# Who begins the base layer's loads: from SyncE's queue to ScalarE's, at the head of its program

## The chip, the cores and the metric

One core of a Trainium2 chip runs the kernel. The metric is the device time in microseconds (us) of one execution; it is given as the median of several runs. The engines are TensorE (PE; its weight loads are PEld), VectorE (DVE), ScalarE (ACT), GpSimd (POOL) and SyncE (SP). "SPq" and "ACTq" are the places where SyncE and ScalarE issue DMAs. The core has 16 DMA engines.

## What is computed

Two layers over x (8 sequences of 512 tokens, 512 wide), each added to its input. The first, cut to what matters:

```python
ae = layernorm(cond, ln_g, ln_b)                 # cond is 8 x 512
h  = gelu(ae @ w1 + b1)
xw = h @ w2 + b2                                 # two factors of rank 8 for each sequence
layer = base_layer[None] + einsum('bdr,bkr->bdk', x_a, x_b)
x = x + (x + einsum('btc,bco->bto', x, layer))
```

The second takes the result: a shared gated network (silu(x w1) * (x w3)) w2, and a router that picks 2 of 8 experts for each token; each expert is gelu(x W1e) W2e. Their weighted sum, divided by 3, is added to x.

`base_layer` is a 512 x 512 matrix in float32 (1 MB). The kernel adds 2 to its diagonal, which takes the two additions of x into the same product.

## The kernel before, in words

Each engine has a program written out by hand, and semaphores tie them together. Every float32 operand of a large product is cut into a high part (a cast to fp32r on ScalarE) and a low part (a subtraction on VectorE); a product is then three matmuls: high by high, low by high, high by low.

Batch b of x is loaded in four tiles of 128 tokens, `xtok[:, t]`, 256 KB each. For each tile TensorE turns it with four transposes (`xtr`, L1478) into a PSUM bank; ScalarE casts that to `xTh` (`xt_hi_`, L799) and VectorE makes `xTl` (`xt_lo_`, L1106). Batch b of the first layer is `base_half(b, o, half)` (L1493 to L1495): for each of four output chunks o, two halves of six matmuls with `bh`, `bl` and the turned x.

The base layer comes in four loads of 256 KB, `basep[:, k]`. VectorE waits for all four (`base_in`), adds 2 to the four diagonal blocks (L1136), ScalarE casts each to `bh` (L838), and VectorE subtracts to get `bl` (L1140). The first half of `base_half(0, 0)` needs all four `xTl` of batch 0 and two `bl`; the second half needs four. Later `turn_base` (L1564) reads `basep` again.

What sets the order around the change:

- SyncE's program begins with three small loads (`craw`, `lng`, `lnb`; L507), then x's four loads of batch 0 (L509), then the four of the base layer (L511), then `w1c` (1 MB), the router weights `rwr`, `rbias`, `b2v` and `cb1T` (L517, L519), the first two 2 MB pieces of `w2c` (L524), the next batch of x (L528), and so on.
- ScalarE's program begins with a square root for the layer norm (L833), before which it loads its function table, and which waits for `stats` from VectorE (`D_VAR`). Then come the four `xt_hi_` of batch 0 and the four casts of `bh`.
- VectorE's program begins with the statistics of `craw` (L1121 to L1123), the reciprocal and two operations on `ae` (L1128 to L1130), the four `xt_lo_` of batch 0, and only then the wait for `base_in`, the four diagonal adds and the four `bl`.
- TensorE's program begins with transposes of `craw` (L1469), the sixteen transposes of batch 0, and `base_half(0, 0)`. The small net on `ae` (L1586) and the conditioning network (`cond_net`, L1555, eight pieces of `w2c`) are put between the following `base_half` calls.
- GpSimd makes constants from `upper` (L702) on once `bl` is there.

Much later, SyncE loads the shared network's weights in pieces of 512 KB into one buffer, `wraw` (L488); ScalarE and VectorE cut each into its parts (L792, L1100) before the next is begun.

Of the kernel before, what the change touches and what calls it, by code (L numbers as in the profile page):

```python
# [14 lines left out]
P = 128  # L15
# [10 lines left out]
def build(nc, x, cond, base, cw1, cb1, cw2, cb2, ln_g, ln_b, rw, rb, w1, w3, w2, w1e, w2e, out):  # L26
    NB, T, D = x.shape
    KC = D // P
    TT = T // P
    HS = w1.shape[1]  # L30
    HC = HS // P
    E, _, HE = w1e.shape
    RK = cw2.shape[1] // (2 * D)
    N = NB * T
# [50 lines left out]
    with ExitStack() as ctx:  # L85
        def sb(name, shape, dt=F32, where=ctx):
            return where.enter_context(nc.sbuf_tensor(name, shape, dt))

        def sem(name):
            return ctx.enter_context(nc.semaphore(name))  # L90
# [113 lines left out]
        with ExitStack() as st:  # L204
# [16 lines left out]
            with ExitStack() as z:  # L221
                basep = sb("basep", [P, KC, D], F32, z)
# [25 lines left out]
        base_in = sem("base_in")  # L248
# [255 lines left out]
        def _(sp):  # L504
# [2 lines left out]
                sp.dma_start(dst, src).then_inc(small_in, 16)  # L507
            for t in range(TT):
                sp.dma_start(xtok[:, t], x_view[:, t, :]).then_inc(x_in[t], 16)  # L509
            for k in range(KC):  # L510
                sp.dma_start(basep[:, k], base[k * P:(k + 1) * P, :]).then_inc(base_in, 16)  # L511
            for dst, src in ((w1c[:], cw1.rearrange("(k p) n -> p k n", p=P)),
                             (rwr[:], rw.rearrange("(k p) e -> p k e", p=P)),
                             (rbias[:], row_bc(rb, P)),
# [273 lines left out]
        def _(act):  # L788
# [39 lines left out]
            def exp_scores(g):  # L828
                act.wait_ge(z_sb, g + 1)
                nc.scalar.activation(ex[:], zx[:], ACT.Exp, scale=-1.0).then_inc(ez, 1)  # L830

            act.wait_ge(d0, D_VAR)
            nc.scalar.activation(stats[:, 9:10], stats[:, 8:9], ACT.Sqrt).then_inc(a0, 1)  # L833
            for t in range(TT):
# [987 lines left out]
```

## Time and profile before

| | us |
|---|---|
| three runs: lowest, median, highest | 1112.78, 1113.86, 1113.91 |
| the profiled execution: span from first to last instruction | 1114.8 |
| TensorE busy in it | 1075.8 (97%) |
| VectorE, ScalarE, GpSimd busy | 483.5, 398.6, 154.2 |
| first base matmul starts | 13.01 |

The profiled execution is one execution; of its own time only the span is shown. It lies 0.9 us above the median of the three runs. Times in the profile count from the span's start. "Busy" of an engine is the time in which it ran instructions other than waits and DMA issues. A row of the timeline gives start, duration, engine, line and operation, and in brackets the idle time before it with what ended it; a row "x4" merges four in a row.

### The profile page before, as it was taken

To read this page: it belongs to the slowest core of one execution; us is meant where nothing else is said; L and a number is where in the kernel's file an instruction comes from. 1 tells how busy PE (TensorE), PEld (TensorE's weight loads), DVE (VectorE), ACT (ScalarE), POOL (GpSimd) and SP (SyncE) were. 2 spreads that over 40 slices of the span, in tenths; PEclk is the share of its full clock that TensorE was granted. 3 is DMA by queue.
4 is the path that set the end of the run, shared out by engine and by line. 5 is a ranking of instruction groups with operands and counts; after the bars stand their busy time and mean duration, and the time that the engine had idled before them with its cause. 6 is when DMAs were issued, how large, how long until landed. Compare 5 with 4: busy or idle time off the path is not lost.

```text
span 1114.8 us, 15416 instructions
## 1 busy us (share of the span) xinstructions
PE 1075.8 (97%) x5226; PEld 878.4 (79%) x5226; DVE 483.5 (43%) x1014; ACT 398.6 (36%) x687; POOL 154.2 (14%) x193
## 2 busy tenths in 40 slices
PE   7999899899699999999999999999999999999998
PEld 5666678688488888888888888888888888888886
DVE  3103654463356646655664533331424333142434
ACT  3212344351366566656656631211212121121211
POOL 2002267370000000000000022011020201102020
PEclk9999899999899999999999999999999999999999
DMA  8662589789768688767657445023050501305041
GB/s 308 263 255 72 187 296 395 277 295 306 204 191 263 210 246 267 223 191 218 203 152 201 174 135 205 1 60 129 0 188 0 188 0 59 130 0 188 0 151 38
DMA packets 131702, 191.42 MB, mean 172 GB/s; under 512 B 9534, under 2 KB 73022, under 8 KB 129878
## 3 DMA queue, kind: packets, MB, share of 16 engines
q1 hardware_dynamic: 120118, 156.38, 43.8%
q0 software_dynamic: 11552, 34.61, 8.3%
q8 instruction: 20, 0.33, 0.1%
q14 instruction: 12, 0.10, 0.0%
HBM read 117.04 MB, written 73.92 MB: 171 GB/s over the span
## 4 chain that ended last, share of the span: by engine, by line
PE 86%; DVE 5%; DMA 4%; SPq 3%; ACT 1%; issue 1%; DVEq 0%; ACTq 0%
PE K L1464 10%; PE K L1465 10%; PE K L1466 10%; PE L L1466 5%; PE L L1464 5%; PE L L1465 5%; PE Rb L1466 5%; PE Rb L1464 5%; PE Rb L1465 5%; PE M L1464 4%; PE M L1466 4%; PE M L1465 4%; PE Rb L1555 3%; PE M L1493 2%; PE M L1495 2%; PE M L1494 2%
## 5 line engine op out<-in xcount | busy, mean ns | idle before, releaser
L462 ACT ACTIVATE slf<-K 128x512 f32<-128x512 f32 x64 | 38.3, 598 | 219.7 <-PE K L1466 219.0
L775 POOL DMA_INDIRECT yb<-ys_d,pos_fix x64 | 61.3, 958 | 321.4 <-DVE total L1395 253.3
L465 ACT CAST gTh<-slf 128x512 fp32r<-128x512 f32 x64 | 39.8, 621 | 183.0 <-DVE slf L475 183.0
L1464 PE MATMUL M<-w2h,gTh 128*128 128x512 f32 x256 | 99.7, 389 | 0.5 <-DVE gTl L477 0.5
L1464 PE MATMUL K<-x1h,w13h 128*128 128x512 f32 x256 | 99.7, 389 | 0.0
L1466 PE MATMUL K<-x1h,w13l 128*128 128x512 f32 x256 | 99.6, 389 | 0.0
L1465 PE MATMUL M<-w2l,gTh 128*128 128x512 f32 x256 | 99.6, 389 | 0.0
L1466 PE MATMUL M<-w2h,gTl 128*128 128x512 f32 x256 | 99.6, 389 | 0.0
L1465 PE MATMUL K<-x1l,w13h 128*128 128x512 f32 x256 | 99.6, 389 | 0.0
L475 DVE TENSOR_TENSOR slf<-L,slf 128x512 f32<-128x512 f32 x32 | 22.1, 691 | 155.9 <-PE L L1466 150.8
L1332 DVE TENSOR_TENSOR e2l<-e2raw,e2h 128x512 fp32r<-128x512 f32 x64 | 41.3, 687 | 79.3 <-ACT e2h L929 79.3
L475 DVE TENSOR_TENSOR slf<-Rb,slf 128x512 f32<-128x512 f32 x32 | 22.1, 691 | 117.8 <-PE Rb L1466 117.8
L754 POOL DMA_INDIRECT xs_d<-x1tok,pos_int x64 | 65.5, 1023 | 35.4 <-issue 18.8
L1336 DVE TENSOR_TENSOR hTl<-hg,hTh 128x512 fp32r<-128x512 f32 x64 | 44.1, 689 | 59.0 <-ACT hTh L945 59.0
L477 DVE TENSOR_TENSOR gTl<-slf,gTh 128x512 fp32r<-128x512 f32 x64 | 44.3, 692 | 47.5 <-ACT gTh L465 47.5
L1493 PE MATMUL M<-xTh,bh 128*128 128x512 f32 x128 | 56.8, 444 | 6.8 <-DVE bl L1140 4.0
L769 POOL COPY pos_fix<-ypos 128x8 int32 (+1 forms) x8 | 1.5, 190 | 446.5 <-DMA ys_d<-yo 405.9
L1464 PE MATMUL K<-x1h,e1h 128*128 128x512 f32 x128 | 50.6, 396 | 11.1 <-DVE x1l L1322 11.1
L1464 PEld LDWEIGHTS M<-w2h,gTh 128*128 128x128 f32 x256 | 48.1, 188 | 10.9 <-DVE gTl L477 1.0
L1466 PEld LDWEIGHTS K<-x1h,w13l 128*128 128x128 f32 x256 | 48.1, 188 | 10.0
L1466 PEld LDWEIGHTS M<-w2h,gTl 128*128 128x128 f32 x256 | 48.0, 188 | 10.0
L1465 PEld LDWEIGHTS K<-x1l,w13h 128*128 128x128 f32 x256 | 48.1, 188 | 9.9
(248 smaller groups left out, 2469.4 us busy)
## 6 DMA issues: line engine op xcount, KB each, us to landing
w2c<-in_L_cond_w_dram SPq DMA_DIRECT2D x8, 2048.0 KB, 8.4
e1raw<-in_L_cond_W1e_dram SPq DMA_DIRECT2D x16, 1024.0 KB, 7.2
e2raw<-in_L_cond_W2e_dram SPq DMA_DIRECT2D x16, 1024.0 KB, 5.6
xr<-xs_d SPq DMA_DIRECT2D x64, 256.0 KB, 4.6
ys_d<-yo SPq DMA_DIRECT2D x32, 512.0 KB, 7.3
xtok<-in_x_dram SPq DMA_DIRECT2D x32, 256.0 KB, 7.4
x_d<-x1tok SPq DMA_DIRECT2D x8, 1024.0 KB, 8.1
xs_d<-zeros SPq DMA_DIRECT2D x8, 1024.0 KB, 8.4
```

The costliest lines, as they stand in the source:

```text
L462: nc.scalar.activation(slf[:, h % 2], U[h % 2][:], ACT.Silu).then_inc(ffn.silu, 1)
L465: nc.scalar.copy(gTh[:, h % 2], slf[:, h % 2]).then_inc(ffn.g_hi, 1)
L475: nc.vector.tensor_tensor(slf[:, h % 2], V[h % 2][:], slf[:, h % 2], ALU.mult).then_inc(ffn.g_f, 1)
L477: nc.vector.tensor_tensor(gTl[:, h % 2], slf[:, h % 2], gTh[:, h % 2].bitcast(F32), ALU.subtract).then_inc(ffn.g_lo, 1)
L754: pool.indirect_dma_start(out=xs_d, out_offset=bass.IndirectOffsetOnAxis(ap=pos_int[:, c:c + 1].bitcast(U32), axis=0), in_=x1tok[i][:, t, ...
L775: pool.indirect_dma_start(out=yb[:, c, :], out_offset=None, in_=ys_d, in_offset=bass.IndirectOffsetOnAxis(ap=pos_fix[:, c:c + 1].bitcast(U ...
L1332: tt(e2l[:, m], e2raw[:, m], e2h[:, m].bitcast(F32), ALU.subtract).then_inc(e2_lo, 1)
L1336: tt(hTl[:, m], hg[:, m % 2], hTh[:, m].bitcast(F32), ALU.subtract).then_inc(ht_lo, 1)
L1464: mm(o, ah, bh_, start=start, stop=False)
L1465: mm(o, ah, bl_, start=False, stop=False)
L1466: return mm(o, al, bh_, start=False, stop=stop)
L1493: mm(bank[:], bh[:, c, cols], xh[:, c], start=(c == 0), stop=False)
```

## The change

The loop of four `dma_start` for `basep` is taken out of SyncE's program, where it stood between x's loads and `w1c`, and put at the head of ScalarE's program, ahead of the wait for `stats` and the square root. Sources, destinations and the semaphore are the same.

```diff
@@ block.sync
             for t in range(TT):
                 sp.dma_start(xtok[:, t], x_view[:, t, :]).then_inc(x_in[t], 16)
-            for k in range(KC):
-                sp.dma_start(basep[:, k], base[k * P:(k + 1) * P, :]).then_inc(base_in, 16)
             for dst, src in ((w1c[:], cw1.rearrange("(k p) n -> p k n", p=P)),
@@ block.scalar
+            for k in range(KC):
+                act.dma_start(basep[:, k], base[k * P:(k + 1) * P, :]).then_inc(base_in, 16)
             act.wait_ge(d0, D_VAR)
             nc.scalar.activation(stats[:, 9:10], stats[:, 8:9], ACT.Sqrt).then_inc(a0, 1)
```

The head of ScalarE's program in the changed kernel (the first row is the jump into the program):

```order
L785 UNCONDITIONAL_BRANCH
L831 DMA basep<-in_L_cond_base_layer_dram 128x512 x4
L833 ACT_TABLE_LOAD
L833 ACTIVATE stats<-stats 8x1
L797 CAST xTh<-K 128x4x128 x2
L797 CAST xTh<-M 128x4x128 x2
```

The four issues stand ahead of the table load, and the rest of ScalarE's rows follow in their old order; the line numbers between the two places of the edit are lower by two.

The head of SyncE's program as a difference:

```order
 L507 DMA lnb<-in_L_cond_ln_b_dram 8x512
 L509 DMA xtok<-in_x_dram 128x512 x4
-L511 DMA basep<-in_L_cond_base_layer_dram 128x512 x4
-L517 DMA w1c<-in_L_cond_w_dram 128x4x512
-L517 DMA rwr<-in_L_cond_router_W_dram 128x8x8
+L515 DMA w1c<-in_L_cond_w_dram 128x4x512
+L515 DMA rwr<-in_L_cond_router_W_dram 128x8x8
```

On SyncE `w1c` now follows x's four loads directly, and all that stands behind it moves up by the four issues. The rows of TensorE and VectorE are the same in both kernels.

## Rows read from the trace of the kernel before

**Rows 1.** The page: span, busy time of each engine, and the chain's shares.
```profile
span 1114.8 us, 15416 instructions
...
PE 1075.8 (97%) x5226; PEld 878.4 (79%) x5226; DVE 483.5 (43%) x1014; ACT 398.6 (36%) x687; POOL 154.2 (14%) x193
...
PE 86%; DVE 5%; DMA 4%; SPq 3%; ACT 1%; issue 1%; DVEq 0%; ACTq 0%
```

**Rows 2.** The chain in order of time, 0 to 60 us: start, duration, what.
```profile
1.93 0.36 SPq L509
...
3.75 0.43 SPq L511
...
5.18 5.39 DMA basep<-n_L_cond_base_layer_dram
10.59 0.30 DVE basep L1136
10.92 0.63 ACT bh L838
11.57 1.30 DVE bl L1140 x2
13.01 0.76 PE M L1493
13.77 0.43 PE M L1494
...
17.18 0.24 PE M L1493
17.42 0.23 PE M L1494
...
21.17 4.04 PE L L1586 x32
```

**Rows 3.** The timeline of ScalarE and VectorE from 0 to 14 us.
```profile
0.80 1.28 ACT L833 ACT_TABLE_LOAD   x1 [0.80 <-PEq L1809]
...
3.19 0.68 DVE L1121 BATCH_NORM_STATS2 stats<-craw 8x6 f32<-8x512 f32 x1 [3.19 <-DMA lnb<-in_L_cond_ln_b_dram]
...
4.28 0.20 ACT L833 ACTIVATE stats<-stats 8x1 f32<-8x1 f32 x1 [2.20 <-DVE stats L1123]
...
9.65 0.69 DVE L1106 TENSOR_TENSOR xTl<-M,xTh 128x512 fp32r<-128x512 f32 x1 [0.44 <-ACT xTh L799]
10.59 0.90 DVE L1136 SCALAR_TENSOR_TENSOR basep<-ident,basep 128x128 f32<-128x128 f32 x4 [0.25 <-DMA basep<-n_L_cond_base_layer_dram]
```

**Rows 4.** The line L509, x's first four loads: durations and landing times of the issues.
```profile
L509 SPq DMA_DIRECT2D xtok<-in_x_dram x4: 360/427/432, 1.9 to 3.3; - x4
...
DMA to landing us min/median/max: 2.5/3.3/4.6
```

**Rows 5.** Busy time by stretch; the last two columns are DMA share and GB/s.
```profile
0.00:3.00 3.00, 0.00 (x0) 0.00 (x0) 0.00 (x0) 1.28 (x1) 0.83 (x7) 1.00 0.06 22
3.00:8.00 5.00, 3.76 (x17) 2.90 (x18) 3.93 (x9) 1.48 (x4) 0.00 (x0) 1.00 0.97 294
8.00:12.00 4.00, 0.99 (x4) 0.59 (x4) 2.71 (x7) 2.16 (x5) 0.00 (x0) 1.00 1.01 378
```

**Rows 6.** The timeline of SyncE's issues behind the base layer's.
```profile
5.65 0.44 SPq L517 DMA_DIRECT2D w1c<-in_L_cond_w_dram  x1
...
6.68 3.28 SPq L517 DMA_DIRECT2D rbias<-_L_cond_router_bias_dram  x1
...
13.10 1.06 SPq L524 DMA_DIRECT2D w2c<-in_L_cond_w_dram  x2
```

**Rows 7.** TensorE's waits from 13 to 110 us: total, times, longest.
```profile
PE M L1493 <- DVE xTl L1106: 2.8, 2, 1.6
PE L L1523 <- DVE zz L1207: 0.7, 1, 0.7
PE M L1505 <- DVE stk L1112: 0.5, 1, 0.5
```

**Rows 8.** Busy time from 24.9 to 33.7 us (granted clock third from last).
```profile
24.90:33.70 8.80, 8.80 (x38) 6.40 (x38) 1.75 (x9) 0.82 (x2) 0.00 (x0) 0.67 0.94 363
```

**Rows 9.** The chain in order of time, 100 to 300 us: two waits for weight pieces.
```profile
195.74 7.93 DMA wraw<-in_L_cond_w_dram
...
240.93 3.82 DMA wraw<-in_L_cond_w_dram
```

## The prediction

> **What bounds the kernel now.** I began with the page: 1114.8 us of span, TensorE busy 97% of it, and a chain that ended last with 86% on PE and 4% on DMA [rows 1]. So a change in loads can only count where TensorE stands idle, or where its start is set by a load. I then read the chain in order of time over the first 60 us [rows 2]. It begins with SyncE's issues, and its longest piece is the flight of the last `basep` load: issued at 5.18, landed 5.39 us later, at 10.57. VectorE's first diagonal add follows at 10.59, ScalarE's first `bh` cast at 10.92, two `bl` subtractions at 11.57, and the first base matmul at 13.01. So the base layer is the last thing that TensorE's first long run waits for.
>
> The next question is who was second. The timeline [rows 3] shows VectorE's last `xTl` of batch 0 running from 9.65 to 10.34, and then an idle time of only 0.25 before the diagonal add. VectorE takes all four `xTl` before it asks for `basep`, so x's path was late too: had `basep` been there long before, the add could have run at 10.34 and no sooner. From one x load to TensorE's start the steps are fixed: the last x load lands at 3.28 + 4.6 = 7.88 [rows 4], the last `xTl` ends at 10.34 (2.46 later), and from the add to the first base matmul is 13.01 - 10.59 = 2.42. With X for the landing of the last x load and both otherwise ready, the matmul starts at X + 2.46 + 2.42 = X + 4.88, so 12.76 with X as it is. **The whole gain that the change can fetch here is 13.01 - 12.76 = 0.25 us**, and it turns into a loss as soon as X is later than 8.13.
>
> **What moves X.** The DMA engines are the point. From 3 to 8 us their mean busy share is 0.97, at 294 GB/s, and from 8 to 12 us 1.01 [rows 5]; before 3 us it is 0.06. x's four loads and base's four are 256 KB each. In the old order x is ahead and base behind. The change lets base in first: ScalarE's first instruction, its table load, is at 0.80 [rows 3], so I let the first base issue begin there, while x's first issue stays at 1.93 [rows 2]. The eight loads took from 1.93 (first issue) to 10.57 (last landing), 8.64 us, with the engines full. The same eight begun at 0.80 end at 0.80 + 8.64 = 9.44, if they move at the same rate. Base has 1.13 us of lead, so x ends last: X = 9.44. That is 1.56 later than 7.88, and the first base matmul stands at 9.44 + 4.88 = 14.32, against 13.01: **1.31 us later**.
>
> The trace never has two hardware queues with loads at once, so X is bounded. Lower end: x is not slowed at all, X = 7.88, a gain of 0.25. Upper end: base is served in full before x, or the issues of the two engines hold each other up so that the lead is lost; then x takes the place that base had and X = 10.57, a start at 15.45, 2.44 later. I take 9.44, which lies nearer the upper end, because the row from 3 to 8 us shows no free engine time that could carry the second stream.
>
> Here the Trainium skill has a rule that speaks against the change. Its page "DMA: Bandwidth & Descriptors", section "Issuing engines are not separate DMA queues", says that DMAs begun by different engines run on the same 16 engines and interleave, and that a second issuing engine saves only issuing time. By that rule x and base share from the moment that both are queued, a second queue adds no rate, and rival 1 below falls away; the sum stays at 1115.2. Rows 5 agree as far as they go (0.97 and 1.01 of the engines busy from one queue); no row of this trace shows the sharing itself.
>
> **The other parts of the edit.**
> - *Four issues added on ScalarE.* On SyncE they run from 3.75 to 5.65, when the next issue starts [rows 2, 6]: 1.90 for four. On ScalarE that is 0.80 to 2.70, then the table load of 1.28 until 3.98. The square root waited until 4.28 for VectorE [rows 3], so 0.30 of cover is left and the cost is nothing. Bounds: below, none; above, if one issue takes the 3.28 of `rbias` [rows 6] instead of 0.43, the table load ends at 6.83 and the square root 2.6 late. VectorE's reciprocal and two `ae` operations then end near 8.6, and four `xTl` of 0.7 near 11.4, under the 11.9 (9.44 + 2.46) at which x lets them end anyway. Still nothing.
> - *cond and the two layer-norm rows* (three 16 KB loads, landed at 3.19 [rows 3]) now share with up to one base load ahead: 256 KB at 294 GB/s is 0.9 us. VectorE's short chain would end at 6.9 instead of 6.0, while its later `xTl` wait for x. Nothing.
> - *Four issues gone from SyncE.* Everything behind x is begun 1.90 earlier: `w1c` at 3.75 instead of 5.65, then the small loads, the first `w2c` at 11.2 instead of 13.10 [rows 6]. `w1c` stands behind x on the same queue, so it cannot delay x; it can take time from base, which has its lead. Earlier arrival is worth nothing: TensorE's waits from 13 to 110 us add up to 4.0 us, all for VectorE, none for a DMA [rows 7].
> - *Work behind the late start.* TensorE has nothing else queued ahead of that matmul, and GpSimd's constants and ScalarE's first `xp` copy follow it. Since rows 7 hold no wait with slack for a load, 1.31 us at the start is not absorbed before 110 us, and later TensorE is again the chain. So it goes through one for one.
> - *Clock.* The first base matmuls follow each other by 0.43, that of 17.18 and those behind it by 0.23 to 0.24 [rows 2]: the faster pace comes 4.2 us after the start. With a later start it comes later by about as much. The granted clock is 0.67 in the mean from 24.9 to 33.7 [rows 8], so part of that stretch runs at 1.2 GHz and the rest at 2.4, after the 4.04 us of small matmuls of L1586. Both move along; I put zero, and 2.9 us to either side as the bound (0.33 of the clock withheld over 8.8 us).
>
> **Sum.** +1.31 (X later by 1.56, less the 0.25 that is won) and zero for the rest. On the profiled execution that is 1114.8 to 1116.1; its span is 0.9 above the median of the three runs, so on the median: 1113.86 + 1.31 = 1115.2 us, or +0.12%.
>
> **Rivals.**
> 1. *The cover holds* (0.20): X stays within 0.2 of 7.88, since two queues draw more from the engines than one. For it: 378 GB/s from 8 to 12 us against 294 before, so some rate was unused. Gain 0.25, time 1113.6.
> 2. *x behind all of base* (0.15): X = 10.57 or later; 1113.86 + 2.44 = 1116.3, slower by 0.22%. Place: the transposes of batch 0. It decides from X = 10.36 on, where the loss is 2.23. For it: base has issues 0.47 apart, faster than 256 KB move (0.87 at 294 GB/s), so by x's first issue more than two base loads are queued. Against: x's later loads would have to gain nothing from the lead.
> 3. *A collision further on goes away* (0.05): the chain from 195.74 waits 7.93 us for a `wraw` piece, while a like wait at 240.93 is 3.82 [rows 9]. If the shift of 1 to 2 us lets that piece through at the lower price, 4.1 is won: 1113.86 + 1.31 - 4.11 = 1111.1. The other direction, a like collision more, is as thinly founded: 0.03, at 1119.3.
> 4. *The change does not do what it says* (0.10): ScalarE's queue begins late, base arrives about when it did, X moves by less than 0.3; 1113.9.
>
> The forecast itself (X between 8.1 and 10.36) has 0.47.
>
> **How the numbers follow.** A measurement of this kernel can tell about 0.2% from no change, which is 2.2 us: under 1111.6 is faster, over 1116.1 slower. Slower: rival 2 and the extra collision, 0.18. Faster: rival 3, 0.05. The rest, 0.77, is within. The likeliest time is 1115.2. The range goes from rival 1 with half of the spread of the runs shown (1113.6 - 0.6 = 1113.0) to rival 2 with as much (1116.3 + 0.6, about 1116.9).
>
> **What would show it.** In the profile after: four `basep` issues on ScalarE's queue before its table load, the first at about 0.8; base landed by about 8; the last x load landed near 9.4, its slowest from 4.6 to about 6.2 us in flight; VectorE's last `xTl` near 11.9; its diagonal add straight behind, with no wait for a DMA; the first base matmul near 14.3. TensorE's waits from there to 110 us should still be about 4 us. I am wrong in size if the last x load lands at 8 or after 10.4, wrong in the order if the diagonal add still waits for `basep`, and wrong about the rest of the kernel if the start moves by one amount and the end by another.

## The result and the profile after

The changed kernel took 1117.83 us in the median of 15 runs (1113.32 to 1120.76); the kernel before, in the same comparison, 1113.91 (1111.54 to 1117.37, 15 runs). The ratio is 1.0032, with a 95% interval of 1.0020 to 1.0045: slower by 3.6 us, 2.2 to 5.0. The forecast was 1115.2, with 1116.9 as the upper end.

The profiled execution is one of the slower ones (1120.76 us, of which its span is 1119.0; so 1.76 us lie around the span, and the profiled execution of before had some 1116.6, by the same allowance, which is 2.7 above the median of the three runs and not the 0.9 that the prediction took for it).

The chain in order of time, changed kernel, first 16 us (start, duration, what; it answers to [rows 2]):

```profile
1.93 5.71 DMA xtok<-in_x_dram
...
7.68 2.22 PE K L1478 x8
9.91 1.72 PE M L1478 x8
...
11.65 0.59 ACT xTh L797
...
12.27 0.69 DVE xTl L1106
12.96 0.21 DVE basep L1136
...
13.19 0.63 ACT bh L838
...
13.84 1.31 DVE bl L1140 x2
...
15.28 0.72 PE M L1493
```

The head of the chain has changed hands. It was the flight of the last `basep` load; now it is the flight of x's first load, issued at 1.93 as before and landed 5.71 us later, at 7.64. Behind it stand all sixteen transposes of batch 0, from 7.68 to 11.63, with one pause of 0.39 us, for the second tile (a line of the timeline shows it):

```profile
8.79 0.71 PEld L1478 LDWEIGHTS K<-ident,xtok 128*128 128x128 f32 x4 [0.39 <-DMA xtok<-in_x_dram]
```

The first base matmul is 2.27 us later than in [rows 2].

The lines of the loads, with the times from issue to landing (they answer to [rows 4]); first L509, x, then L831, base:

```profile
L509 SPq DMA_DIRECT2D xtok<-in_x_dram x4: 360/427/432, 1.9 to 3.3; - x4
...
DMA to landing us min/median/max: 5.7/6.4/6.6
...
L831 ACTq DMA_DIRECT2D basep<-n_L_cond_base_layer_dram x4: 392/452/453, 0.8 to 2.2; - x4
...
DMA to landing us min/median/max: 2.8/3.6/6.4
```

x's loads were in flight for 2.5 to 4.6 us and are now for 5.7 to 6.6, though they are issued at the same times. Taken one by one, the tiles land at 7.6, 8.8, 9.2 and 9.9. The timeline of the same stretch shows what else was late:

```profile
2.67 1.28 ACT L833 ACT_TABLE_LOAD   x1 [2.67 <-issue]
...
4.52 0.68 DVE L1121 BATCH_NORM_STATS2 stats<-craw 8x6 f32<-8x512 f32 x1 [4.52 <-DMA lnb<-in_L_cond_ln_b_dram]
...
12.87 0.89 DVE L1136 SCALAR_TENSOR_TENSOR basep<-ident,basep 128x128 f32<-128x128 f32 x4
...
13.67 2.13 SPq L526 DMA_DIRECT2D xtok<-in_x_dram  x4
```

The small loads land 1.33 us later than in [rows 3]. The diagonal add has no idle time before it: base is no longer waited for. Behind the start nothing is new. TensorE's waits up to 112 us, to be read against [rows 7]:

```profile
PE M L1493 <- DVE bl L1140: 3.7, 1, 3.7
PE M L1493 <- DVE xTl L1106: 2.8, 2, 1.6
PE L L1523 <- DVE zz L1207: 0.7, 1, 0.7
PE M L1505 <- DVE stk L1112: 0.5, 1, 0.5
```

Apart from the first, which is the start itself, these are the rows of before to the tenth. The late start is carried along: the weight piece that was waited for from 195.74 on in [rows 9] is now waited for from 197.91, 2.17 later:

```profile
197.91 8.00 DMA wraw<-in_L_cond_w_dram
...
243.41 4.84 DMA wraw<-in_L_cond_w_dram
```

That row alone proves little: in late4 below, whose start is 1.78 late, it stands at 195.00. Behind it this pair of executions parts further, to 2.48 at the second of these rows and 4.2 at the end, all of it before 400 us: from there on TensorE is busy without a pause in both, at a granted clock of 1.00. Whether that belonged to the change was the open question of the experiments.

### The profile page after: what moved, and what is told of

It is laid out like the page before. It is cut to its first block, busy times and chain, and to the rows that moved or that the text cites. A ratio compares the mean times of both kernels' runs of the same rounds, so it can differ in the third digit from the quotient of the medians.

```text
span 1119.0 us, 15416 instructions
## 1 busy us (share of the span) xinstructions
PE 1076.6 (96%) x5226; PEld 879.3 (79%) x5226; DVE 483.4 (43%) x1014; ACT 398.3 (36%) x687; POOL 155.4 (14%) x193
## 4 chain that ended last, share of the span: by engine, by line
PE 86%; DVE 5%; DMA 4%; SPq 3%; ACT 1%; issue 1%; DVEq 0%; ACTq 0%
PE K L1464 10%; PE K L1465 10%; PE K L1466 10%; PE L L1464 5%; PE L L1465 5%; PE L L1466 5%; PE Rb L1465 5%; PE Rb L1464 5%; PE Rb L1466 5%; PE M L1464 4%; PE M L1465 4%; PE M L1466 4%; PE Rb L1555 3%; PE M L1493 2%; DMA wraw<-in_L_cond_w_dram 2%; PE M L1494 2%
## 5 line engine op out<-in xcount | busy, mean ns | idle before, releaser
L1464 PEld LDWEIGHTS K<-x1h,w13h 128*128 128x128 f32 x256 | 48.1, 188 | 9.9
```

What stands on the lines that cost most here:

```text
L1464: mm(o, ah, bh_, start=start, stop=False)
```

## The experiments

Three theories were there to be told apart. **Bytes ahead**: base's bytes are moved ahead of x's, whichever queue they come from, and the late start goes through one for one. **The queue**: a second hardware queue costs something by itself. **Amplified**: a late start costs more than itself later on. "Start" is the first base matmul in the run's profile. In before it was at 13.01, and in a second profile of the same kernel (`null`, below) at 12.71. Runs were compared with before on the same chip; two of the chips were slower as a whole (before at about 1136 us), so only ratios compare across them.

| run | start | ratio to before, 95% | in us |
|---|---|---|---|
| the change | 15.28 | 1.0032 (1.0020 to 1.0045) | +3.6 |
| after_again | 14.81 | 1.0014 (0.9999 to 1.0029) | +1.6 |
| after_third | 15.59 | 1.0029 (1.0006 to 1.0052) | +3.3 |
| hold_w1c | 15.29 | 1.0032 (1.0017 to 1.0046) | +3.6 |
| swap_sp | 16.11 | 1.0031 (1.0014 to 1.0049) | +3.5 |
| late4 | 14.79 | 1.0020 (1.0007 to 1.0032) | +2.2 |
| late4_again | 14.65 | 1.0016 (0.9996 to 1.0037) | +1.8 |
| late7us | 19.38 | 1.0042 (1.0024 to 1.0059) | +4.8 |
| half_act | 13.37 | 1.0003 (0.9989 to 1.0016) | +0.3 |
| base_act_late | 12.85 | 1.0003 (0.9990 to 1.0016) | +0.3 |
| rbias_act | 12.85 | 0.9991 (0.9978 to 1.0004) | -1.0 |
| rbias_again | 13.29 | 0.9998 (0.9974 to 1.0022) | -0.2 |
| small_act | 12.82 | 1.0005 (0.9991 to 1.0019) | +0.6 |
| x_act | 12.51 | 1.0012 (0.9997 to 1.0027) | +1.3 |
| small_act_ln_late | 12.71 | 0.9982 (0.9958 to 1.0006) | -2.0 |
| x_first | 12.46 | 1.0042 (1.0018 to 1.0067) | +4.8 |
| null | 12.71 | 0.9988 (0.9966 to 1.0011) | -1.4 |

**The order without the queue.** `swap_sp`:

```diff
-            for t in range(TT):
-                sp.dma_start(xtok[:, t], x_view[:, t, :]).then_inc(x_in[t], 16)
             for k in range(KC):
                 sp.dma_start(basep[:, k], base[k * P:(k + 1) * P, :]).then_inc(base_in, 16)
+            for t in range(TT):
+                sp.dma_start(xtok[:, t], x_view[:, t, :]).then_inc(x_in[t], 16)
```

> The kernel before with the base layer's four loads ahead of x's four, both still on SyncE: the order of the change without its second queue and without its head start. Theory 'bytes ahead' (x is late because base's bytes are moved first): the first x tile lands at about 7.7 or a little later, the last at about 10.6, TensorE's sixteen transposes follow in one run, and the first base matmul stands at 15.3 to 16.3, 2.3 to 3.3 us late, the median over before by at least as much. Rival 'two queues hinder each other': x's first tile lands earlier than in the change (under 7.0), and the start is less late than the change's 2.27.

Timeline of TensorE and VectorE in `swap_sp`:

```profile
8.76 1.97 PE L1478 MATMUL K<-ident,xtok 128*128 128x128 f32 x8 [4.78 <-DMA xtok<-in_x_dram]
...
13.70 0.89 DVE L1136 SCALAR_TENSOR_TENSOR basep<-ident,basep 128x128 f32<-128x128 f32 x4
...
16.11 0.77 PE L1493 MATMUL M<-xTh,bh 128*128 128x512 f32 x1 [3.67 <-DVE bl L1140]
```

The expectation's 7.7 for the first x tile was too early (8.7), its start was met. Here TensorE waits for no later tile, and the sixteen transposes take 3.68 us, 8.76 to 12.44. One queue with base in front starts 0.8 us later than two, so the second queue does not hinder x and base: the change's head start of 1.13 us is worth most of itself, and the order costs 3.1.

**The queue without the order.** `base_act_late` keeps base on ScalarE but behind x's first tile:

```diff
             nc.scalar.activation(stats[:, 9:10], stats[:, 8:9], ACT.Sqrt).then_inc(a0, 1)
+            act.wait_ge(x_in[0], 16)
+            for k in range(KC):
+                act.dma_start(basep[:, k], base[k * P:(k + 1) * P, :]).then_inc(base_in, 16)
```

and on SyncE base's loop goes out and `sp.wait_ge(x_in[TT - 1], 16)` stands ahead of `w1c`.

> Base's four loads on ScalarE's queue, but begun only when x's first tile has landed (behind the square root); SyncE begins w1c when x's last tile has landed. Same queue as in the change, the order of before. Theory 'order, not queue': x lands as before (last at about 7.9 or a little later), base's last at 11.3 to 11.8 since its first issue is at 4.5 instead of 3.75, first base matmul at 13.8 to 14.3, median 0.8 to 1.4 over before. Rival 'the queue costs 1 us or more by itself': the same start and the median 2 to 3 over before.

```profile
4.45 1.86 ACTq L835 DMA_DIRECT2D basep<-n_L_cond_base_layer_dram  x4
...
10.44 0.90 DVE L1138 SCALAR_TENSOR_TENSOR basep<-ident,basep 128x128 f32<-128x128 f32 x4 [0.77 <-DMA basep<-n_L_cond_base_layer_dram]
```

The start was better than expected: base was issued 0.70 later than in before and landed no later (the diagonal add that waits for it began at 10.44, against 10.59), probably because `w1c` was held back; that was not tried alone. The time is that of before (+0.3 us, -1.1 to 1.8). With the same queue and the same bytes, only behind x, the loss does not show.

`rbias_act` puts one 4 KB load that nobody waits for early, `rbias`, at the head of ScalarE, and nothing else; it was run twice:

> The kernel before with one 4 KB load that nothing early waits for (rbias) begun by ScalarE at the head of its program; x and base stay as they were on SyncE. Theory 'a second hardware queue costs something by itself' (the three kernels with loads on ScalarE's queue stood 1.1 to 1.8 us above what their start explains): start within 0.4 us of 13.0 and the median 1.0 to 1.8 over before. Rival 'it costs nothing, the excess is the clock's stretches and chance': median within 0.7 of before.

> rbias_act once more; it stood 1.6 us (0.3 to 2.9) under before with a start only 0.16 early. Theory 'scatter': mean within 0.8 of before. Rival 'taking rbias out of SyncE's line is worth 1.5 us': 1.0 to 2.0 under before again.

A price of 1 us or more for the second queue does not show: -1.0 us (-2.5 to 0.4) and -0.2 us (-3.0 to 2.5). The first of the two hinted at a gain, the second did not repeat it.

**Half of it.** `half_act` has base's loads 0 and 1 on ScalarE at the head, 2 and 3 on SyncE behind x.

> Base's loads 0 and 1 on ScalarE at the head, loads 2 and 3 on SyncE behind x. Half the bytes are ahead of x. Theory 'bytes ahead': x's first tile lands near 6, the last near 9.0, the last xTl at 11.4 to 12.0, first base matmul at 13.8 to 14.4 (about half of the change's 2.27 late), median 1 to 2 over before. Rival 'any load on the other queue stops x until it is through': x's first tile after 7.0 and the start over 1.8 late.

```profile
6.08 1.97 PE L1480 MATMUL K<-ident,xtok 128*128 128x128 f32 x8 [0.51 <-DMA xtok<-in_x_dram]
...
13.37 0.77 PE L1495 MATMUL M<-xTh,bh 128*128 128x512 f32 x1 [3.67 <-DVE bl L1142]
```

x's first transposes began at 6.08, the start was at 13.37, earlier than expected, and the time is that of before, where 1 to 2 us more was expected. So it is not so that any load on the other queue stops x; half the bytes ahead of x move x's first tile by 1.6 us, and 0.36 of that reaches the start, because the rest falls into the time in which base was waited for anyway and into pauses between the four tiles. (0.36 is hardly more than the 0.30 by which the two starts of the kernel before differ.)

**What moved up on SyncE.** `hold_w1c` is the change with `sp.wait_ge(x_in[TT - 1], 16)` ahead of `w1c`.

> The changed kernel, but SyncE waits for the last tile of x before it begins w1c and all behind it: takes away what the moved-up loads could do to x and base. Theory 'w1c is behind x on its queue and costs it nothing': first and last x tile land as in the change (near 7.6 and 9.9), start near 15.3, median within 0.7 us of the change's. Rival 'w1c takes its share out of x': x's last tile lands at 9.4 or earlier and the start is 0.5 us or more earlier than the change's 15.28.

Start 15.29 against 15.28, and the same +3.6 us: the loads that moved up on SyncE cost and bring nothing that shows.

**A late start with all loads as they were.** `late4`:

```diff
                 act.wait_ge(diag, k + 1)
+                for i in range(4 if k == 0 else 0):
+                    nc.scalar.copy(x1tok0[:, i], basep[:, k])
                 nc.scalar.copy(bh[:, k], basep[:, k]).then_inc(base_hi, 1)
```

> The kernel before, loads as they were, with four extra 128x512 copies on ScalarE ahead of the first bh cast (0.61 us each in the trace of before), so that the first base matmul is 2.4 to 2.5 us late for a reason that has nothing to do with DMA. Theory A (the late start is the whole cause, and what the change lost beyond its 2.27 us of start was added later by the shift itself): the first base matmul near 15.5 and the median 3.5 to 4 us over before, as the change's. Theory B (a late start goes through one for one, the rest of the change's loss comes from the moved transfers or from a noisy median): the start as late, the median 2.3 to 2.6 over before.

> The four extra copies on ScalarE again: a start 1.8 to 2.4 us late with all loads as before; both theories: mean 1.3 to 3.0 over before. It is the yardstick for after_third.

```profile
10.62 2.17 ACT L839 COPY x1tok<-basep 128x512 f32<-128x512 f32 x4 [1.06 <-DVE basep L1138]
...
14.79 0.77 PE L1495 MATMUL M<-xTh,bh 128*128 128x512 f32 x1 [5.85 <-DVE bl L1142]
```

The first run's start stood at 14.79 and not near 15.5; the four copies in a row took 2.17 us.

`late7us` does the same with ten copies, each waiting for the one before:

> The kernel before with ten extra copies on ScalarE, one after the other, ahead of the first bh cast: a start about 7 us late (0.6 to 0.8 us each), with all loads as before. Theory 'a late start goes through one for one': the mean over before equals the shift of the first base matmul in the profile within 1.2 us. Rival 'a late start is amplified by half' (as the change's 3.4 for 2.27 would have it): the mean 1.4 to 1.6 times the shift, 10 to 11 us.

Against a mean start of 12.86 in the two profiles of before, late4's starts (14.79, 14.65) are 1.86 late for a time of +2.1, and late7us's 19.38 is 6.5 late for +4.8 (2.7 to 6.7). Nothing is amplified. late7us's time is 1.7 us short of its shift, more than the 1.2 that was allowed; the interval still reaches the shift, so that a part of a long delay is won back is possible and not shown.

**The change twice more, and before against itself.**

> The changed kernel once more. Its mean stood 3.4 us (2.2 to 4.5) over before, its start 2.27. Theory 'the start is all, the rest is the scatter of single executions': the start again at 15.2 to 15.4, the mean over before 2.0 to 3.0. Rival 'something later in the change costs another 1 us': the mean 3.1 or more over before again.

> The kernel before, submitted against itself. Theory 'scatter': the means differ by up to 1 us though nothing differs, and the first base matmul stays within 0.4 us of 13.0. If they agree within 0.3 us, the excess of the change is unlikely to be scatter.

> The changed kernel a third time. Theory 'the start is all': start 1.8 to 2.4 us late, mean over before 1.3 to 3.0 and within 1 us of late4_again's. Rival 'a fixed part beyond the start': mean 3.0 or more over before and over 1 us more than late4_again's.

Both repeats missed what was expected of them, on either side. after_again started at 14.81, not at 15.2 to 15.4, and stood 1.6 us over before, not 2.0 to 3.0. after_third stood 3.3 over before and 1.5 more than late4_again, with a start 0.9 later than late4_again's: by the letter that was the rival's case, a fixed part beyond the start. Each of these two comparisons is uncertain by more than 2 us, so they do not decide it.

Weighted by their intervals, the three comparisons of the change give 1.0025, or +2.8 us with 1.8 to 3.8, for starts that are 2.4 late in the mean. The excess over the start, 0.4 with an uncertainty of 1.0, is nothing that can be told from zero; a fixed part of up to 1.4 us is not ruled out either. `null`, the same kernel on both sides, stood 1.4 us apart with an interval of plus and minus 2.6. In the medians of a dozen runs on these chips 1 us is scatter.

Where a part of the scatter comes from shows in two profiles of nearly the same kernel: before with a span of 1114.8, and `rbias_act` with 1106.6. Busy time by stretch, granted clock third from last; first before, then rbias_act:

```profile
12.00:34.00 22.00, 20.99 (x100) 16.77 (x104) 4.59 (x15) 4.59 (x9) 7.17 (x16) 0.84 0.95 344
...
107.00:195.00 88.00, 79.87 (x402) 63.89 (x403) 52.31 (x182) 38.23 (x67) 45.02 (x56) 0.94 0.76 282
```

```profile
12.00:34.00 22.00, 21.16 (x157) 16.38 (x158) 4.45 (x15) 4.79 (x8) 7.16 (x16) 0.92 0.95 346
...
107.00:195.00 88.00, 80.02 (x432) 64.63 (x432) 50.64 (x177) 38.83 (x68) 44.60 (x56) 1.00 0.83 303
```

The granted clock is 0.92 in one and 0.84 in the other from 12 to 34 us, and 1.00 and 0.94 from 107 to 195. What that is worth shows in a stretch of the same work: from the first base matmul to the first product of the conditioning network (`Rb`, L1555) TensorE has 48 base matmuls, the small net and a dozen small matmuls, and no wait. Two rows of before, then two of rbias_act (start and duration first):

```profile
25.63 0.63 PE L1494 MATMUL M<-xTl,bh 128*128 128x512 f32 x1
...
33.67 3.92 PE L1555 MATMUL Rb<-w2c,hTz 128*32 128x128 f32 x64
```

```profile
24.14 0.40 PE L1494 MATMUL M<-xTl,bh 128*128 128x512 f32 x1
...
30.00 3.92 PE L1555 MATMUL Rb<-w2c,hTz 128*32 128x128 f32 x64
```

Before needs 20.66 us for it (13.01 to 33.67), rbias_act 17.15 (12.85 to 30.00). The twelve base matmuls behind the small net start 0.43 us apart in before, at 1.2 GHz (granted clock 0.50 from 24 to 28 us), and 0.23 apart in rbias_act, at 2.4 GHz (1.00); and the first fast matmul comes 4.0 us after the start in one and 2.7 in the other. The same weight piece is then waited for at 195.74 and at 187.28.

The changed kernel shows it in its own profiles, after and after_again:

```profile
35.84 3.92 PE L1555 MATMUL Rb<-w2c,hTz 128*32 128x128 f32 x64
```

```profile
31.94 3.92 PE L1555 MATMUL Rb<-w2c,hTz 128*32 128x128 f32 x64
```

From their starts that is 20.56 and 17.13 us, and 20.39 in after_third. The chip is not the reason: on one and the same chip after_again needed 17.13 and rbias_again 20.69. So an execution of the changed kernel can be 1.7 us ahead of the profiled one of before at this point, though it started 1.8 later. How much of the head of the program runs at 1.2 GHz and how much at 2.4 differs from one execution to the next by more than the change is worth; what decides it was not tried.

**Can the head be shortened at all?** The first attempt was the change turned round: x on ScalarE, base on SyncE.

> x's four loads of batch 0 on ScalarE's queue at the head, base's four on SyncE behind the three small loads. Theory 'bytes ahead': x's first tile lands near 3.3, the last by 7.9 or earlier, base's last at 9.4 to 9.7 instead of 10.57; first base matmul at 11.9 to 12.2, 0.8 to 1.1 early, median 0.8 to 1.1 under before or a little more. Rival 'the small loads pay': cond and the layer-norm rows land over 1 us later and hold the square root and VectorE's first operations, so that the last xTl is no earlier than 10.3; gain under 0.3 at the start.

```profile
0.80 1.84 ACTq L831 DMA_DIRECT2D xtok<-in_x_dram  x4
...
4.75 0.68 DVE L1121 BATCH_NORM_STATS2 stats<-craw 8x6 f32<-8x512 f32 x1 [4.75 <-DMA lnb<-in_L_cond_ln_b_dram]
4.86 0.56 PE L1469 MATMUL L<-ident,craw 8*128 8x8 f32 x4 [4.86 <-DMA lnb<-in_L_cond_ln_b_dram]
...
5.36 1.97 PE L1478 MATMUL K<-ident,xtok 128*128 128x128 f32 x8
...
10.10 0.89 DVE L1136 SCALAR_TENSOR_TENSOR basep<-ident,basep 128x128 f32<-128x128 f32 x4
```

The start was only 0.5 early, and the time did not follow it (+1.3 us, -0.3 to 3.0). The rival was right in its cause, with TensorE held as well as VectorE: the three small loads landed after 4.7, and both engines take them first. (It had put the last `xTl` no earlier than 10.3; it ended at 10.18.) The transposes of x stood ready behind those of `craw` until 5.36. `small_act` puts the small loads on ScalarE and x first on SyncE:

> The three small loads (craw, lng, lnb) on ScalarE's queue at the head; SyncE begins with x and goes on with base, 1.12 us earlier than before. Theory 'bytes ahead, in x's order': x's first tile lands near 3.4, base's last at 9.5, first base matmul at 11.9 to 12.1, about 1 us early, median 0.7 to 1.3 under before. Rival 'second queue costs 1 us or more': the start as early, the median equal to before. Rival 'small loads late': they land after 4.4 behind x's first tile, the square root and VectorE's first operations end after 7.6, and the last xTl and with it the start are less than 0.5 us early.

They landed late again (4.87), start 12.82, as its third theory had it. `small_act_ln_late` also moves three of VectorE's operations behind the `bl`:

> small_act, with VectorE's reciprocal and first two ae operations moved from ahead of batch 0's four xTl to just ahead of the third ae operation. Theory 'in small_act and x_act the late small loads held the xTl': the last xTl ends at 9.0 to 9.5, the diagonal add waits for base's last load (9.1 to 9.4), first base matmul at 11.5 to 12.0, 1.0 to 1.5 us before the old one, the mean 0.8 to 1.6 under before. Rival 'the earlier start is lost again to the clock or to the layer norm's later end': the start as early and the mean within 0.5 of before.

The last `xTl` ended at 10.38, not at 9.5, because TensorE still took `craw` first; start 12.71, and an interval that reaches from 0.9958 to 1.0006. `x_first` cleared that too; on each engine x's batch 0 stands ahead of the layer norm. TensorE's part of the edit:

```diff
-            pe.wait_ge(small_in, 16 * 3)
-            for k in range(KC):
-                last_mm = turn8(L, 0, craw, k)
-            last_mm.then_inc(p0, 1)
             for t in range(TT):
                 xtr(0, t)
+            pe.wait_ge(small_in, 16 * 3)
+            for k in range(KC):
+                last_mm = turn8(L, 0, craw, k)
+            last_mm.then_inc(p0, 1)
```

> Small loads on ScalarE's queue; x, then base, at the head of SyncE; and on every engine the work on x's batch 0 ahead of the layer norm's (TensorE's transposes of craw, VectorE's copy and its ae operations, ScalarE's square root go behind it). Theory 'it was the small loads, which TensorE and VectorE take first': first transposes of x at 3.5 to 4.0, last xTl at 7.8 to 9.2, the diagonal add waits for base's last load (9.1 to 9.6), first base matmul at 11.5 to 12.1, mean 0.5 to 1.8 under before. Rival 'the time comes back at the net': the layer norm ends too late for the small net (L1586), which then starts no earlier than before (21.0), and the mean is within 0.5 of before.

Timeline of `x_first`:

```profile
3.71 1.96 PE L1478 MATMUL K<-ident,xtok 128*128 128x128 f32 x8 [3.71 <-DMA xtok<-in_x_dram]
...
9.66 0.90 DVE L1130 SCALAR_TENSOR_TENSOR basep<-ident,basep 128x128 f32<-128x128 f32 x4
...
12.46 0.77 PE L1493 MATMUL M<-xTh,bh 128*128 128x512 f32 x1 [3.59 <-DVE bl L1134]
...
13.84 5.75 DVE L1139 TENSOR_SCALAR ae<-craw,stats 8x512 f32<-8x512 f32 x1
...
21.07 0.59 PE L1469 MATMUL L<-ident,ae 8*128 8x8 f32 x4 [3.48 <-DVE ae L1141]
```

The add stood at 9.66 at last and the start at 12.46, still 0.4 short of what was expected: the square root's table load (1.28 us at 8.98) now held the `bh` casts. And then the layer norm was late: TensorE waited 3.48 us for `ae`, and the small net began at 26.88 instead of 21.01. The rival held, and more than held: +4.8 us. No version beat the kernel before beyond doubt.

## Why the prediction was wrong

- **What bounds the head: right.** Base was the last, x second, with 0.25 us between them; the whole gain to be had was those 0.25, and x turned it into a loss. Half_act and base_act_late show both sides of it.
- **"The eight loads end at 9.44, base has the lead, x ends last": right in kind, 0.44 short.** The last x load landed at 3.28 + 6.6 = 9.88, inside the forecast's own bracket (8.1 to 10.36). Begun 1.13 us earlier, the eight loads took 9.1 us and not 8.64: the rate of the old order did not carry over. That w1c took its share is excluded by hold_w1c, whose last x load landed no earlier.
- **"The matmul starts at X + 4.88": the step that failed.** The 4.88 was read from a trace in which the first x tile came at 4.5 and TensorE's transposes kept pace with the loads; there only the last tile counts. In the change the first tile lands at 7.64, the second at 8.8, and the other two come closer together than TensorE turns a tile (0.92 us each in swap_sp), so they queue up: the transposes end at 11.63, the last `xTl` at 12.96. From the last landing to there it is 3.08 us and not 2.46; from there to the first base matmul 2.32 and not 2.42, as nothing is waited for in between. The start is 0.96 us later than the 14.32 forecast: 0.44 from the landing, 0.62 from the queue of tiles, less 0.10. I had asked when the last byte of x comes and not when the first does, though the first is what the other queue's lead holds back most: 3.2 us against 2.0 for the last.
- **The clock, put at zero with 2.9 us to either side: not contradicted, and left out of the range.** In this pair the stretch behind the start is the same (20.66 and 20.56 us); in after_again it is 17.13. The term does not belong to the change, but two executions can differ by 3.5 us in it.
- **ScalarE's four issues, SyncE's moved loads, the order of the diagonal add: right.** The table load ended at 3.95; hold_w1c stood where the change did; no DMA was waited for at 12.87. The small loads were 1.33 late where 0.9 was put, and in this kernel it cost nothing, as said. In x_act and small_act it was the bound.
- **One for one: right within the uncertainty of 1 us**, by the three comparisons of the change and by late4. By late7us a start 6.5 late costs 4.8 (2.7 to 6.7).
- **Rival 2** had nearly the size of the start (2.44 against 2.27) by luck, since its condition (X of 10.36 or later) was not met and its place was wrong: not the last tile behind all of base, but the first tile behind most of it (base's last load landed at 2.2 + 6.4 = 8.6). The prediction gave 0.18 to a slower kernel.
- **The range** ended at 1116.9 since both the start and the scatter were put too small: 0.6 us on either side, half of the spread of three runs. Fifteen runs of before spread over 5.8 us. With the start as it was, 1113.9 + 2.3 = 1116.2 would have been the forecast, and the measured 1117.8 lies 1.6 above it; the comparison's own interval (2.2 to 5.0) just reaches the start, null shows such a distance to be possible by chance, and where these 1.6 us come from stays open. Of the 2.6 us by which the forecast time was missed, only 1.0 is the start's.

The page "DMA: Bandwidth & Descriptors" of the Trainium skill (section "Issuing engines are not separate DMA queues") had it that a second issuing engine saves issuing time and no transfer time; swap_sp and the change agree: the start is at 16.11 from one queue and at 15.28 from two, 0.83 us earlier, which is less than the 1.13 us by which the first issue came earlier.

## What to carry to other kernels

When a load is let in front of another, ask when each piece of the one behind will come, the first above all, and what serial work (here sixteen transposes, 4 us) hangs on the first pieces; the last byte's time is only enough while the consumer keeps pace. A load that is waited for last by 0.25 us is worth 0.25 us, however long the wait for it looks in the chain. And where single executions scatter by 5 us, a shift of 2 can be read from one profile at its place of origin (13.01 against 15.28) and nowhere behind it; what reaches the end takes dozens of runs and an equal delay made by other means beside it.

## What the runs showed that was not expected

- The three small loads (16 KB each, issued from 0.81 to 1.60) landed at 3.19 in before and after 4.2 (up to 4.9) in every profile in which ScalarE had issued any load at the head, even with `rbias` alone, 4 KB (4.22 and 4.24). With base in front on SyncE's own queue (swap_sp) it was 3.31, and with base on ScalarE but begun at 4.45 (base_act_late) 3.35. So what does not cost the whole kernel anything that shows does cost these loads 1 us; why was not tried.
- An 8x512 tensor_scalar on VectorE that takes 0.53 us elsewhere (at 13.86 in small_act_ln_late) took 5.75 in x_first, from 13.84 to 19.59, while GpSimd ran its memsets back to back from 14.15 to 19.65. In small_act_ln_late two VectorE tensor_tensor of the same size (at 14.43 and 15.14) took 0.68 each beside the first of the same memsets, so not every operation is held. That the long one and the memsets belong together is argued from the times, not shown.
